# Layers 2 and 3 of a four-layer kernel: the inverse applied once a tile, the triangle made transposed

## The reference, cut to what matters

```
k = x / norm(x);  v = (x @ W_write.T) * beta;  k_beta = k * beta
A0 = tril(-(k_beta @ k.T * L), -1);  A = inverse(eye - A0)       # per chunk
v = A @ v;  k_cumdecay = A @ (k_beta * decay_exp)
def step(S, (k_i, v_i, kcd_i)):
    v_new = v_i - kcd_i @ S
    o_i = (k_i * de) @ S + tril(k_i @ k_i.T * L) @ v_new
    S = chunk_total_decay * S + (k_i * dw).T @ v_new
out + o @ W_read.T
```

```
S = a * (S - b * outer(S @ k, k)) + b * outer(v, k);  o = q @ S
```

## Time and profile before

| | |
|---|---|
| median of 3 runs | 1829.18 us (1828.34 to 1829.65) |
| the profiled execution | 1830.12 us, of which span 1828.3 us |
| granted PE clock, mean | 0.996 |
| busy share of the span | PE 96%, POOL 64%, DVE 70%, ACT 59% |

### The profile page before, as it was taken

One profiled execution on the slowest core, in us unless ns is written; L12 is line 12 of the kernel. 1 busy time (PEld: TensorE's weight loads), 2 busy tenths in 40 slices (PEclk: granted clock), 3 DMA queues, 4 the chain that ended last, 5 costly groups with the idle time before them and its releaser, 6 DMA issues.

```text
span 1828.3 us, 31828 instructions
## 1 busy us (share of the span) xinstructions
PE 1759.1 (96%) x10270; PEld 1338.7 (73%) x10270; DVE 1274.2 (70%) x4547; ACT 1082.8 (59%) x2686; POOL 1177.2 (64%) x1547
## 2 busy tenths in 40 slices
PE   7999999999999999999999999999998999999988
PEld 5788988866676666666666676677878887788874
DVE  7863345688869887888889765546557766678684
ACT  5554226566676577777676775456545556544555
POOL 5555658888878877878778863134437664454456
PEclk9999999999999999999999999999999999999999
DMA  6100000010000000000000000000000000000002
GB/s 241 65 25 1 1 3 2 3 48 1 1 2 1 1 1 1 1 1 1 1 1 1 6 5 5 1 1 8 3 1 3 11 21 17 20 2 1 2 9 62
DMA packets 24473, 26.44 MB, mean 14 GB/s; under 512 B 3492, under 2 KB 21284, under 8 KB 23924
## 3 DMA queue, kind: packets, MB, share of 16 engines
q1 hardware_dynamic: 24308, 24.41, 4.1%
HBM read 22.26 MB, written 2.15 MB: 13 GB/s over the span
## 4 chain that ended last, share of the span: by engine, by line
PE 79%; DVE 8%; POOL 6%; ACT 4%; issue 2%; DMA 1%; SPq 0%; POOLq 0%; DVEq 0%; ACTq 0%
PE ps L86 72%; PE ps L89 7%; POOL arena L103 5%; ACT arena L97 4%; DVE arena L103 3%; DVE arena L143 1%; DVE arena L106 1%; DVE arena L109 1%; DVE arena L126 1%; ACT L97 0%; DMA cst<-in_cst 0%; DVE arena L123 0%; DVE arena L129 0%; DVE arena L112 0%; DVE ps L143 0%
## 5 line engine op out<-in xcount | busy, mean ns | idle before, releaser
L103 POOL TENSOR_TENSOR arena<-arena 128x128 f32<-128x128 f32 (+6 forms) x796 | 693.5, 885 | 348.0 <-DVE arena L103 127.5
L97 ACT ACTIVATE arena<-ps 128x128 f32<-128x128 f32 (+13 forms) x1100 | 352.8, 354 | 435.2 <-PE ps L86 312.6
L86 PE MATMUL ps<-arena 128*128 128x128 f32 (+4 forms) x2864 | 460.3, 295 | 18.6 <-DVE arena L103 11.5
L86 PEld LDWEIGHTS ps<-arena 128*128 128x128 f32 x2864 | 381.4, 192 | 118.3 <-issue 63.1
L103 DVE TENSOR_TENSOR arena<-ps,arena 128x128 f32<-128x128 f32 (+4 forms) x696 | 319.1, 470 | 179.4 <-PE ps L86 162.8
L97 ACT ACTIVATE arena<-arena 128x128 f32<-128x128 f32 (+1 forms) x772 | 299.8, 442 | 35.3 <-POOL arena L103 27.5
L97 ACT ACTIVATE arena<-ps,cols 128x512 f32<-128x512 f32 x324 | 218.3, 689 | 170.9 <-PE ps L86 156.0
L86 PE MATMUL ps<-arena,cst 128*128 128x504 f32 (+2 forms) x768 | 289.2, 493 | 8.2 <-POOL arena L103 3.1
L86 PE MATMUL ps<-arena,moe 128*128 128x256 f32 (+1 forms) x960 | 289.7, 441 | 0.6 <-DVE arena L103 0.6
L89 PE MATMUL ps<-cst,arena 128*128 128x128 f32 (+1 forms) x1392 | 238.4, 275 | 14.8 <-ACT arena L97 6.3
L109 DVE SCALAR_TENSOR_TENSOR arena<-ps,arena 128x128 f32<-128x128 f32 (+2 forms) x424 | 141.9, 373 | 131.0 <-PE ps L86 87.1
(11 more groups left out here) (110 smaller groups left out, 1847.6 us busy)
## 6 DMA issues: line engine op xcount, KB each, us to landing
rows<-in_rows SPq DMA_DIRECT2D x1, 2253.0 KB, 15.1
arena<-in_x SPq DMA_DIRECT2D x8, 256.0 KB, 5.0
wf<-in_wf SPq DMA_DIRECT2D x2, 1024.0 KB, 5.9
arena<-in_L_ffn_W SPq DMA_DIRECT2D x8, 256.0 KB, 3.2
out_dram<-arena SPq DMA_DIRECT2D x8, 256.0 KB, 2.8
wmod<-in_wmod SPq DMA_DIRECT2D x4, 384.0 KB, 7.7
arena<-kept SPq DMA_DIRECT2D x24, 64.0 KB, 2.8
arena<-kept SPq DMA_DIRECT2D x8, 192.0 KB, 3.1
```

The costliest lines, as they stand in the source:

```text
L86: return UNSENT if self.e is None else self.e.matmul(out, lhsT, rhs, start=start, stop=stop)
L97: return self.e.activation(out, in_, func, bias=bias, scale=scale)
L103: return UNSENT if self.e is None else self.e.tensor_tensor(out, a, c, op)
```

## The change

- W_read is multiplied into W_write at the start (`wwr`: one matmul and one copy), so values, state and output of layer 2 are already those that W_read would give. `d2r` and `oT` go.
- In both layers the right side is built first and the inverse applied once. `d2c` (`e3c`) is now keys times state; DVE makes w = v − decay·(k·S) from it (`w`); `d2u` is one product, XT·w. beta moves from the rows to the columns of the triangle, that is, behind the inverse: it multiplies u when u is copied (ACT for layer 2's `vn`, DVE for layer 3's `u`). `kb` and `akt` go.
- In layer 2 the product of keys and state also serves the output: ACT copies it, times the decay, from the bank of `d2c` to `kS`, and POOL adds it to h. The product S·kTg and `kTg` go. The state's addition is made ahead of the output, in a bank of its own (`d2s`; in layer 3 `e3r`, with `e3Rt` and `e3ut` for the transposes and `e3p` for the old `e3w`).
- The triangle is made transposed (`above`), directly where the inversion works; in layer 3 POOL makes `above` from `DT` by a subtraction of 128x512 for each group. Layer 3's `e3d` transposes go. At level 0 of the inversion, PE's transposes and ACT's copy are replaced by a transpose of 32x32 blocks on DVE (`tr32`), whose entries that the mask keeps lie inside such blocks. Levels 1 to 6 stay.
- kd (keys times decay) gets two buffers in both layers, and moves from DVE to ACT in layer 3.
- The digits of all four `TURNS` strings are other ones, over the whole kernel: 3108 for PE (3122 before), 3740 for DVE (3842), 1997 for ACT (2031), 1044 for POOL (1066).

The diff's core (strings of digits, layout and the scalings on DVE left out):

```diff
+            ps = banks.take(pe, b, b, "wwr")
+            pe.wait_ge(*arrives("sm"))
+            pe.mm(ps[:, 0:128], wsm("ww2")[:, 0:128], wsm("wread")).then_inc(*pe.up(b, "wwr"))
...
+            ps = banks.get(b, "wwr")
+            dve.wait_ge(*at("wwr"))
+            dve.cp(wsm("ww2")[:, 0:128], ps[:, 0:128]).then_inc(*dve.up(b, "writeread", free=(b, "wwr")))
...
+        BLOCKWISE = (0,)
+
         def inv_pe(b, m, *key):
             for n in range(7):
-                ps = banks.take(pe, b, b, "inv_f", n, *key)
-                if n:
+                if n not in BLOCKWISE:
+                    ps = banks.take(pe, b, b, "inv_f", n, *key)
                     pe.wait_ge(*at("inv_v", b, n, *key))
-                else:
-                    pe.wait_ge(*at("inv_m", b, *key))
-                for i in range(4):
-                    ins = pe.tr(ps[:, col4(i)], m.G4[:, i, 0:128] if n else m.tri[:, col4(i)], ident)
-                ins.then_inc(*pe.up(b, "inv_f", b, n, *key))
-                yield
+                    for i in range(4):
+                        ins = pe.tr(ps[:, col4(i)], m.G4[:, i, 0:128], ident)
+                    ins.then_inc(*pe.up(b, "inv_f", b, n, *key))
+                    yield
                 ps = banks.take(pe, b, b, "inv_p", n, *key)
-                if n == 0:
-                    pe.wait_ge(*at("inv_v", b, 0, *key))
+                pe.wait_ge(*at("inv_v", b, n, *key))
                 pe.wait_ge(*at("inv_y", b, n, *key))
                 pe.wait_ge(*at("inv_r", b, n, *key))
...
-            ps = banks.get(b, "inv_f", 0, *key)
-            act.wait_ge(*at("inv_f", b, 0, *key))
-            act.act(m.M4, four(ps[:, :])).then_inc(*act.up(b, "inv_v", b, 0, *key, free=(b, "inv_f", 0, *key)))
...
+            for n in range(7):
+                yield
+                if n in BLOCKWISE:
+                    if n:
+                        dve.wait_ge(*at("inv_p", b, n - 1, *key))
+                    dve.wait_ge(*at("inv_v", b, n, *key))
+                    dve.tr32(four(m.Y), m.M4).then_inc(*dve.up(b))
+                    dve.wait_ge(*dve.last(b))
+                    dve.tt(four(m.Y), four(m.Y), over(neg(n)), ALU.mult).then_inc(*dve.up(b, "inv_y", b, n, *key))
...
+            pool.wait_ge(*at("inv_t", b, *key))
+            pool.tt(m.M4, m.M4, over(ident), ALU.subtract).then_inc(*pool.up(b, "inv_v", b, 0, *key))
...
                         ps = banks.take(pe, b, b, "d2c", t)
-                        pe.wait_ge(*at("inv_x", b, "l2", g))
-                        pe.wait_ge(*at("d2kb", b, t))
-                        pe.mm(ps[:, 0:128], m.kb, m.XT[:, c]).then_inc(*pe.up(b, "d2c", b, t))
+                        pe.wait_ge(*at("d2S", b, t - 1))
+                        pe.mm(ps[:, 0:128], m.kT[:, c], m.S).then_inc(*pe.up(b, "d2c", b, t))
                     yield
                     ps = banks.take(pe, b, b, "d2u", t)
                     pe.wait_ge(*at("inv_x", b, "l2", g))
-                    ins = pe.mm(ps[:, 0:128], m.XT[:, c], m.vb[:, c], start=True, stop=(t == 0))
                     if t:
-                        pe.wait_ge(*at("d2akt", b, t))
-                        pe.wait_ge(*at("d2S", b, t - 1))
-                        ins = pe.mm(ps[:, 0:128], m.akt, m.S, start=False, stop=True)
-                    ins.then_inc(*pe.up(b, "d2u", b, t))
+                        pe.wait_ge(*at("d2w", b, t))
+                    pe.mm(ps[:, 0:128], m.XT[:, c], m.w if t else m.vb[:, c]).then_inc(*pe.up(b, "d2u", b, t))
+                    yield
+                    pe.wait_ge(*at("d2vn", b, t))
+                    if t < NT - 1:
+                        ps = banks.take(pe, b, b, "d2s", t)
+                        pe.wait_ge(*at("d2kd", b, t))
+                        pe.mm(ps[:, 0:128], m.kds[t % 2], m.vn).then_inc(*pe.up(b, "d2s", b, t))
                     yield
                     ps = banks.take(pe, b, b, "d2o", t)
-                    pe.wait_ge(*at("d2vn", b, t))
                     if i == 0:
                         pe.wait_ge(*at("d2am", b, g))
-                    pe.wait_ge(*at("d2kd", b, t))
-                    ins = pe.mm(ps[:, 0:128], m.vn, m.gram[:, c], start=True, stop=(t == 0))
-                    if t:
-                        pe.wait_ge(*at("d2kTg", b, t))
-                        ins = pe.mm(ps[:, 0:128], m.S, m.kTg, start=False, stop=True)
-                    if t < NT - 1:
-                        ins = pe.mm(ps[:, 128:256], m.kd, m.vn)
-                    ins.then_inc(*pe.up(b, "d2o", b, t))
-                    yield
-                    ps = banks.take(pe, b, b, "d2r", t)
-                    pe.wait_ge(*at("d2oT", b, t))
-                    pe.mm(ps[:, 0:128], m.oT, wsm("wread")).then_inc(*pe.up(b, "d2r", b, t))
...
+                    if t > 1:
+                        act.wait_ge(*at("d2s", b, t - 2))
+                    if t < NT - 1:
+                        act.act(m.kds[t % 2], m.kk[:, c], scale=dec2[:, 127:128]).then_inc(*act.up(b, "d2kd", b, t))
                     if t:
-                        act.wait_ge(*at("d2r", b, t - 1))
-                    act.act(m.kd, m.kk[:, c], scale=dec2[:, 127:128]).then_inc(*act.up(b, "d2kd", b, t))
-                    if t:
                         yield
                         ps = banks.get(b, "d2c", t)
-                        act.wait_ge(*at("d2c", b, t))
-                        act.act(m.akt, ps[:, 0:128], scale=-1.0).then_inc(
-                            *act.up(b, "d2akt", b, t, free=(b, "d2c", t)))
-                    yield
-                    ps = banks.get(b, "d2o", t)
-                    act.wait_ge(*at("d2o", b, t))
-                    act.act(m.oT, ps[:, 0:128]).then_inc(
-                        *act.up(b, "d2oT", b, t, free=(b, "d2o", t) if t == NT - 1 else None))
+                        act.wait_ge(*at("d2w", b, t))
+                        if t > 1:
+                            act.wait_ge(*at("d2hk", b, t - 1))
+                        act.act(m.kS, ps[:, 0:128], scale=m.gcol).then_inc(
+                            *act.up(b, "d2kS", b, t, free=(b, "d2c", t)))
+                    yield
+                    ps = banks.get(b, "d2u", t)
+                    act.wait_ge(*at("d2u", b, t))
+                    act.act(m.vn, ps[:, 0:128], scale=m.bt[:, i:i + 1]).then_inc(
+                        *act.up(b, "d2vn", b, t, free=(b, "d2u", t)))
...
-                        dve.wait_ge(*at("d2r", b, t - 1))
-                    if i == 0:
-                        dve.wait_ge(*at("d2am", b, g))
-                    dve.ts(m.kb, m.kk[:, c], m.bg[:, i:i + 1], None, ALU.mult).then_inc(*dve.up(b, "d2kb", b, t))
-                    yield
-                    ps = banks.get(b, "d2u", t)
-                    dve.wait_ge(*at("d2u", b, t))
-                    dve.cp(m.vn, ps[:, 0:128]).then_inc(*dve.up(b, "d2vn", b, t, free=(b, "d2u", t)))
+                        ps = banks.get(b, "d2c", t)
+                        dve.wait_ge(*at("d2c", b, t))
+                        dve.stt(m.w, ps[:, 0:128], m.ngcol, m.vb[:, c], ALU.mult, ALU.add).then_inc(
+                            *dve.up(b, "d2w", b, t))
...
-                pool.wait_ge(*at("d2tri", b, g))
-                pool.tt(four(m.tri), four(m.tri), over(ident), ALU.subtract).then_inc(
-                    *pool.up(b, "inv_m", b, "l2", g))
-                yield
                 yield from inv_pool(b, m, "l2", g)
                 for i in range(4):
                     t = 4 * g + i
                     c = col4(i)
+                    pool.wait_ge(*at("d2ho", b, t))
                     if t:
-                        pool.wait_ge(*at("d2r", b, t - 1))
-                        pool.tt(m.kTg, m.kT[:, c], dec2[:, 128:256], ALU.mult).then_inc(*pool.up(b, "d2kTg", b, t))
-                    yield
-                    pool.wait_ge(*at("d2ho", b, t))
+                        pool.wait_ge(*at("d2kS", b, t))
+                        pool.tt(m.h[:, c], m.h[:, c], m.kS, ALU.add).then_inc(*pool.up(b, "d2hk", b, t))
+                        pool.wait_ge(*pool.last(b))
...
-                ps = banks.take(pe, b, b, "e3d", g)
-                for i in range(4):
-                    ins = pe.tr(ps[:, col4(i)], m.DT[:, col4(i)], ident)
-                ins.then_inc(*pe.up(b, "e3d", b, g))
...
+                        pe.wait_ge(*at("e3R", b, t - 1))
+                        pe.mm(ps[:, 0:128], m.kT[:, c], m.R).then_inc(*pe.up(b, "e3c", b, t))
+                        ps = banks.take(pe, b, b, "e3Rt", t)
+                        pe.tr(ps[:, 0:128], m.R, ident).then_inc(*pe.up(b, "e3Rt", b, t))
                     yield
                     ps = banks.take(pe, b, b, "e3u", t)
-                    ins = pe.mm(ps[:, 0:128], m.XT[:, c], m.vb[:, c], start=True, stop=(t == 0))
+                    pe.wait_ge(*at("inv_x", b, "l3", g))
                     if t:
-                        pe.wait_ge(*at("e3akt", b, t))
-                        pe.wait_ge(*at("e3R", b, t - 1))
```

(63 more changed lines are left out.)

330 lines of the change are left out of this document (162 added, 168 removed).

## The result

Before, the median is 1829.41 us (1828.34 to 1829.73, 4 runs); after, 1764.66 us (1761.49 to 1764.88, 4 runs). The ratio is 0.9643, 95% interval 0.9626 to 0.9660: 65 us or 3.6% faster. The forecast was 1790 us, and its range ended at 1769. The direction was right and the size too small: 39.5 us was foreseen, 65 came.

What follows compares the result with a forecast made beforehand. PE was taken to set the pace of layers 2 and 3, 92.6% full. Removing 36.6 us of its work, 39.5 us with slack shrinking in proportion, gave 1830.1 − 39.5 = 1790.6, so 1790 us; range 1769 to 1811.

Steps and rivals of the forecast that it cites:

- the sum: Whole kernel: profiled 1830.1 − 39.5 = 1790.6 us, set to 1790 us against the median 1829.18, 2.2% less.
- The new orders may shift the other 1440 us either way: Outside layers 2 and 3: 1050 to 1370 us can gain nothing; elsewhere 5 us either way allowed.
- The prediction's own sign for this case: Stretch up to 1370 us: moving by more than 5 us makes the forecast wrong and points to the orders.
- PE's work: Layers 2 and 3: 327 of 10270 PE instructions go, leaving 9943; 36.6 us at 0.112 us each.
- Let the slack shrink in proportion: 1370 to 1760 us: slack falls along with PE's work, making 36.6/0.926 = 39.5 us of the 36.6.
- gaps take part of it: Rival, layers 2 and 3: half the saving turns into gaps, 1811 us; chance 0.23 for 1798 to 1818.
- the 30 us worked out from the rule of the Trainium skill: Layers 2 and 3: PE 83% full by weight-load time, only that share of 36.6 us gained, 1799 us; chance 0.10.
- Wide instructions: 1370 to 1760 us: priced 0.483 us for 512 columns, 0.236 for 256; PE came out 92.6% full.
- The other engines: Beside PE: DVE 24 us lighter, block transpose 0.72 us each, ACT even, POOL gains 10.2 us; they have room.
- the two new waits: Layers 2 and 3: `e3Rt`'s bank, taken as 0, 8 us kept for the range; kS, covered by other elements' work.

Runs made afterwards that it cites:

- e1: Kernel before, with the changed kernel's order of steps for layers 0 and 1 and its own, shifted, for layers 2 and 3; 1806.82 us, ratio 0.9874.
- e11: Changed kernel with orders reworked, 128 products of layer 1's expert part made once more (256 PE instructions); 1793.89 us, ratio 0.9809.
- e4: Changed kernel with 116 products of layers 2 and 3 made twice into the same bank (232 PE instructions put back); 1780.53 us, ratio 0.9736.
- e12: Changed kernel with the 116 products of e4 each made three times (464 PE instructions put back); 1803.01 us, ratio 0.9856.
- e9: Changed kernel without POOL's addition of kS to h, orders digit for digit those of its reworked control; 1764.86 us, ratio 0.9646.
- e2: Changed kernel, with the order of steps of the kernel before for layers 0 and 1; 1821.97 us, ratio 0.9957.
- e8: As e1, but each element's layer 2 begins where the changed kernel's order has it, fading into the common shift over 250 us; 1849.13 us, ratio 1.0106.
- e3: Changed kernel with level 0's 64 transposes back on PE, those steps put midway between their neighbours in the order; 1780.14 us, ratio 0.9723.
- e10: As e3, but each transposing step stands in PE's order 0.45 us after POOL has the triangle ready; 1776.37 us, ratio 0.9710.
- e6: Changed kernel without POOL's addition of kS to h and ACT's wait for it, orders worked out again; 1782.59 us, ratio 0.9742.

## Why the prediction was wrong, and where it was right

**The step that failed** is in the sum: "The new orders may shift the other 1440 us either way", with 5 us allowed. The mark behind layer 1 came 34 us earlier. The prediction worked out how full PE is for layers 2 and 3 and found 92.6% there, but not for the rest of the kernel. It looked at 1050 to 1370 us by busy time and took that as full, rightly: the slack there is 2.6 us. For all other stretches it allowed 5 us without a look. By start distances 52 us of slack lay between 276 and 1050 us, as much as all that comes behind the last experts. e1 shows that the order alone takes 31 us out of layer 1, with no instruction changed. The prediction's own sign for this case, that the stretch up to 1370 us moves by more than 5 us, came true.

**PE's work** was right to the instruction, 9943, and 36.6 us at 0.112. In a full stretch that price holds (e11: 28.2 of 28.7 us). Not all operands are float32, as was said ahead of the prediction: 75 of the 10270 instructions are bfloat16. None of them is in the count.

**"Let the slack shrink in proportion"** was wrong in sign. It made 39.5 us of 36.6; what came behind the mark of layer 1 was 31 us, since the slack there grew by 4 to 5 us. e4 and e12 fit that, for work put back: in layers 2 and 3 it lies partly over gaps, and costs 0.57 of its price for the first 26 us and 0.87 for the second. The rival "gaps take part of it" has the mechanism that these runs support for these layers, at a seventh of the work rather than half.

By coincidence that is close to the 30 us worked out from the rule of the Trainium skill (Perfetto Trace Analysis, Identifying the Most-Contended Engine) that weight-load time tells better than matmul busy time how near PE is to its peak. The weight-load share of the earlier trace rows, 83%, is still not how full PE was: by start distances it was (146.2 + 205.7)/393 = 90% from 1367.3 to 1760 us, and the experts' stretch has 1.6 us of slack where weight loads fill 115/150 = 77%. Where the page and the measurement differ, the measurement decides. What the rule is right in is that busy time, 97% in layer 1, hid the slack.

**Wide instructions** were priced too high, 0.483 and 0.236 us from busy time over count; start to start they take 0.429 and 0.217. That made PE look 2 points fuller than it was.

**The other engines.** The block transpose takes 0.706 us (0.72 taken). DVE fell by 33.7 us (24 foreseen, with the small operations counted at nothing), POOL rose by 4.5 (10 foreseen). ACT's busy time fell by 23.7 us where it was called even, but its work was even: all durations added up come to 1252.3 us before and 1249.7 after. ACT's instructions overlap in the record, and how much depends on the order: e1, with the instructions of the kernel before and durations of 1251.8 us, is busy for 1072.6 us instead of 1082.8. Of the two new waits, that for kS costs nothing that shows (e9); that for the bank of `e3Rt` no run tests.

**What stays open.** How much of the 31 us behind layer 1 is structure and how much is its own order can't be split by these runs: e2 gives the structure 7 us with a bad seam, e8 shows two orders of these layers 42 us apart. What is shown is the work removed, the slack that stayed, and that layer 1's gain comes from its order; how much of the rest needs an order made for it was not told apart.

## What to carry to other kernels

Where streams of engines are laid out in a fixed order and the order is made anew, the whole kernel is changed, not the part that was edited: work out the slack at full pace for every stretch, from the distances of starts, and let the range reach as far as the largest slack. Work on a busy engine had its full price only where the slack was near nothing; adding removed work back, once and twice, measures this in two runs. When an experiment edits one step of such an order, time a control that went through the same procedure first, and compare its trace stretch by stretch: e3 and e10 differ in a stretch that neither edited.

## What the runs showed of the hardware

- PE's pace is even for a shape: 6163 of the 6604 instructions of 128x128 start 109 to 113 ns before the next one. Two instructions carry a float32 product, and each takes 0.112 us for 128 columns, but also 0.112 us for 64 and 0.112 us for 8 columns (median start to start before the change, 128 instructions of each of the narrow ones): below 128 columns nothing is saved. Full weights of 128 columns are loaded in each case. The 24 instructions of 8 columns whose weights have one column take 0.026 us. 257 columns take 0.217 us against 0.216 for 256.
- 384 columns take 0.163 us in bfloat16 (35 instructions) against 0.323 us in each of the two instructions of a float32 product.
- The same set of instructions took 1806.82 and 1849.13 us in two orders (e1, e8), and other places for 61 digits of POOL, 12 of DVE and 6 of ACT, with PE's order untouched, took 17.7 us (e6, e9).
- The granted clock fell for short spells from 2.4 to 1.2 GHz in some executions and not in others with the same order: at 114 and 162 us in e1 and e3, not in e8 and e10. PE was at work before both: in the 4 us ahead of each it ran 16 instructions of 8 columns among others, in e3 with no hold-up over 0.11 us. The two spells cost 3.6 us together.
